# First attention: head norms summed by TensorE instead of VectorE

## The reference, cut to what matters

```python
xn = layernorm(x)
q = (xn @ Wq.T + bq)            # 16 heads of 16
k = (xn @ Wk.T + bk)            # 8 heads of 16
v = (xn @ Wv.T + bv)            # 8 heads of 16
q, k = rotary(q), rotary(k)     # turns pairs, keeps each head's length
n = sqrt(sum(h * h)) per head   # of q and of k
p = (h / max(n, 1e-6)) @ R.T    # R: 8 x 16, random features
feats = [sin(p), cos(p)] / 4
out = qp @ (kp^T v) per position, over heads
s = out @ Wo.T + bo
```

## Time and profile before

| | us |
|---|---|
| median of 3 runs (lowest, highest) | 1841.6 (1835.0, 1843.4) |
| the profiled execution, its span | 1837.6, 1835.8 |
| first attention, from the start to the last copy out of `psO` | 0 to 319.2 |
| DVE busy over the span | 1380.6 (75%) |
| PE busy over the span, weight loads | 1597.9 (87%), 1238.0 (67%) |

### The profile page before, as it was taken

One profiled execution on the slowest core, in us unless ns is written; L12 is line 12 of the kernel. 1 busy time (PEld: TensorE's weight loads), 2 busy tenths in 40 slices (PEclk: granted clock), 3 DMA queues, 4 the chain that ended last, 5 costly groups with the idle time before them and its releaser, 6 DMA issues. The chain is left out here.

```text
span 1835.8 us, 34559 instructions
## 1 busy us (share of the span) xinstructions
PE 1597.9 (87%) x9650; PEld 1238.0 (67%) x9650; DVE 1380.6 (75%) x3710; ACT 1031.0 (56%) x2457; POOL 667.8 (36%) x842
## 2 busy tenths in 40 slices
PE   6996886689954786999999999996899999988896
PEld 5885765579953563554555555544799999977775
DVE  7899998266657877999888888833666666667777
ACT  2664654256656660566676767674556666543443
POOL 2655687400027623111237667620000000056662
PEclk9998999789986995999999999998999999999998
DMA  9333456644435885432435545413864444355552
GB/s 343 130 87 85 106 146 167 205 137 133 133 116 168 290 306 149 99 74 61 106 97 156 160 142 171 128 61 122 274 201 133 133 134 133 117 166 164 169 165 75
DMA packets 279591, 272.72 MB, mean 149 GB/s; under 512 B 121769, under 2 KB 248426, under 8 KB 277356
## 3 DMA queue, kind: packets, MB, share of 16 engines
q1 hardware_dynamic: 255672, 215.41, 39.8%
q0 software_dynamic: 18432, 50.36, 9.0%
q10 hardware_dynamic: 5332, 4.96, 0.8%
HBM read 136.84 MB, written 133.69 MB: 147 GB/s over the span
## 5 line engine op out<-in xcount | busy, mean ns | idle before, releaser
L1890 ACT ACTIVATE ca_PT<-ca_psS 128x512 f32<-128x512 f32 (+3 forms) x768 | 336.3, 494 | 202.9 <-PE ca_psS L1927 197.8
L1430 POOL DMA_INDIRECT g_y<-ys_scratch,pos x128 | 125.0, 977 | 428.2 <-POOLq L73 357.0
L1806 DVE CUSTOM_DVE_ANT_0 ca_masked_row<-ca_psM,mask_row 128x384 f32<-128x384 f32 (+3 forms) x512 | 224.3, 486 | 44.4 <-PE ca_psM L1910 42.4
L1927 PE MATMUL ca_psS<-ca_QS,ca_KS 128*128 128x512 f32 (+1 forms) x480 | 174.7, 367 | 1.4 <-ACT ca_PT L1890 1.4
L1810 DVE TENSOR_REDUCE ca_part<-ca_psM 128x1 f32<-128x512 f32 x256 | 163.4, 685 | 16.1 <-PE ca_psM L1910 14.7
L1939 PE MATMUL ca_psO<-ca_PT,ca_VA 128*17 128x512 f32 (+3 forms) x1536 | 161.0, 491 | 6.0 <-ACT ca_OT L1882 5.9
L1910 PE MATMUL ca_psM<-ca_KS,ca_QS 126*128 126x512 f32 (+2 forms) x480 | 159.0, 379 | 6.5 <-DVE ca_part L1806 4.2
L797 PE MATMUL fa_psO<-fa_weighed,ident 128*128 128x256 f32 x512 | 127.9, 407 | 38.1 <-DVE fa_weighed L585 38.1
L1927 PEld LDWEIGHTS ca_psS<-ca_QS,ca_KS 128*128 128x128 f32 x480 | 90.2, 189 | 86.8 <-ACT ca_PT L1890 58.1
L391 POOL DMA_INDIRECT xs_scratch<-x_sb,pos x128 | 124.6, 973 | 55.9 <-ACT ca_PT L1890 34.1
L797 PEld LDWEIGHTS fa_psO<-fa_weighed,ident 128*128 128x128 f32 x512 | 101.7, 204 | 59.0 <-DVE fa_weighed L585 44.6
(11 more groups left out here) (271 smaller groups left out, 4638.5 us busy)
## 6 DMA issues: line engine op xcount, KB each, us to landing
xs_scratch<-fa_blank SPq DMA_DIRECT2D x32, 640.0 KB, 4.9
x_sb<-xs_scratch SPq DMA_DIRECT2D x143, 128.0 KB, 2.1
ys_scratch<-x_sb SPq DMA_DIRECT2D x143, 128.0 KB, 1.7
xs_scratch<-fa_blank SPq DMA_DIRECT2D x32, 384.0 KB, 6.4
spare<-qk_scratch SPq DMA_DIRECT2D x24, 512.0 KB
ca_QS<-qk_scratch SPq DMA_DIRECT2D x20, 512.0 KB, 6.1
ca_KS<-qk_scratch SPq DMA_DIRECT2D x20, 512.0 KB, 7.6
x_sb<-in_ffn SPq DMA_DIRECT2D x16, 608.0 KB, 4.5
```

The lines of the kernel that those rows point to most:

```text
L1430: pool.indirect_dma_start(y[:, t % R, k, :], None, y_dram, bass.IndirectOffsetOnAxis(pos[:, t, k:k + 1], 0)).then_inc(got[t % R], 16)
L1806: ins = dve.tensor_tensor_reduce(masked_row[:, (n * NU + u) % BANKS, h * w:(h + 1) * w], bank[:, h * w:(h + 1) * w], mask_row[:, CHUNK - w ...
L1890: act.activation(PT[:, s % PTS, h, off:CHUNK], psS[(GH * s + h) % BANKS][:, off:CHUNK], ACT.Exp)\
L1927: pe.matmul(psS[tile % BANKS][:, off:CHUNK], KS[slot][:, h, kt * P:(kt + 1) * P], QS[slot][:, h, c * CHUNK + off:(c + 1) * CHUNK], start=T ...
```

## The change

DVE's `square_norm` and its buffer `n2` go. ACT's Square moves from `take_qkv`, where it read `psQ`, to `keep_rotT`, where it reads the transposed rotated rows in `psR` right after the copy to `rotT`. PE's `random_projection` issues three more float32 matmuls: the squared transposed rows (128 x 128) against `heads`, a 128 x 8 block matrix of ones, into 24 further columns of `psP`. `keep_p` copies 216 columns instead of 192, and `norm` takes the sums from there and waits for `p_out` instead of `n2_done`. `heads` is made once by DVE, by a reduction of the identity matrix, before its first step. `project` no longer waits for ACT's squares. The diff, cut to its core:

```diff
@@ DVE @@
-            def square_norm(t, i, b):
-                dve.wait_ge(sq_done, t + 1)
-                dve.tensor_reduce(n2[:, i, :], sq[:, i % 2, :].rearrange("p (h d) -> p h d", d=D), AX.X, ALU.add)\
-                   .then_inc(n2_done, 1)
...
+            dve.wait_ge(ident_in, 16)
+            dve.tensor_reduce(heads[:, :], ident[:].rearrange("p (h d) -> p h d", d=D), AX.X, ALU.add).then_inc(heads_done, 1)
             in_steps(dve, (5, bounded_norm), (11, sine_sums), (5, inverse_norm), (8, in_turns), (11, centre), (8, whole_turns), (11, weigh),
-                     (8, fraction), (3, square_norm), (9, differences), first=BESIDE, beside=beside)
+                     (8, fraction), (9, differences), first=BESIDE, beside=beside)
@@ ACT @@
                 act.activation(qk[:, i % 2, :], psQ[:, 0:NQK], ACT.Copy).then_inc(qk_out, 1)
-                if late(t, 2):
-                    act.wait_ge(n2_done, t - 1)
-                act.activation(sq[:, i % 2, :], psQ[:, 0:NQK], ACT.Square).then_inc(sq_done, 1)
...
                 act.activation(rotT[:, i % 2, :], psR[:, 0:NQK], ACT.Copy).then_inc(rotT_out, 1)
+                act.activation(sq[:, i % 2, :], psR[:, 0:NQK], ACT.Square).then_inc(rotT_out, 1)
...
-                act.activation(p_sb[:, i, :, :].rearrange("p h f -> p (h f)"), psP[:, 0:QK_HEADS * RF], ACT.Copy).then_inc(p_out, 1)
+                act.activation(p_sb[:, i, :], psP[:, 0:NP + QK_HEADS], ACT.Copy).then_inc(p_out, 1)
...
-                    act.wait_ge(n2_done, t + 1)
+                    act.wait_ge(p_out, t + 1)
...
-                    act.activation(inv[:, some, :], n2[:, some, :], ACT.Sqrt).then_inc(norm_done, BATCHED)
+                    act.activation(inv[:, some, :], p_sb[:, some, NP:NP + QK_HEADS], ACT.Sqrt).then_inc(norm_done, BATCHED)
@@ PE @@
                 if t >= 1:
-                    pe.wait_ge(sq_done, t)
                     pe.wait_ge(qk_out, t)
...
                 for k in range(NQK // P):
-                    ins = pe.matmul(psP[:, k * 64:(k + 1) * 64], rotT[:, i % 2, k * P:(k + 1) * P], rblk[:],
-                                    start=k == 0, stop=True, skip_group_check=True)
+                    if k == 0:
+                        pe.wait_ge(rotT_out, t * 2 + 1)
+                    pe.matmul(psP[:, k * 64:(k + 1) * 64], rotT[:, i % 2, k * P:(k + 1) * P], rblk[:],
+                              start=k == 0, stop=True, skip_group_check=True)
+                pe.wait_ge(rotT_out, t * 2 + 2)
+                for k in range(NQK // P):
+                    at = NP + k * QHEADS
+                    ins = pe.matmul(psP[:, at:at + QHEADS], sq[:, i % 2, k * P:(k + 1) * P], heads[:, :],
+                                    start=False, stop=True, skip_group_check=True)
                 ins.then_inc(p_done, 1)
```

More of the change, by code:

```diff
@@ L415, in first_attention @@
         v = sb("v", [P, TILES, NV])
-        n2, inv = sb("n2", [P, POS_TILES, QK_HEADS]), sb("inv", [P, POS_TILES, QK_HEADS])
-        p_sb = sb("p_sb", [P, POS_TILES, QK_HEADS, RF])
+        NP, QHEADS = QK_HEADS * RF, P // D
+        inv = sb("inv", [P, POS_TILES, QK_HEADS])
+        p_sb, heads = sb("p_sb", [P, POS_TILES, NP + QK_HEADS]), sb("heads", [P, QHEADS])
         turns, whole = (sb(x, [P, 2, QK_HEADS, RF]) for x in ("turns", "whole"))
@@ L428, in first_attention @@
         (eps_done, root_done, rstd_done, xn_done, xT_done, hi_done, lo_done, logits_out, whi_done, wlo_done, qk_done, qk_out, v_done,
-         v_out, bias_part, rot_parts, rot_done, sq_done, n2_done, norm_done, norm_part, inv_done, rotT_done, rotT_out, p_done, p_out,
+         v_out, bias_part, rot_parts, rot_done, heads_done, norm_done, norm_part, inv_done, rotT_done, rotT_out, p_done, p_out,
          turns_part, turns_done, apart_done, sine_done, sines_done, A_done, centred, weighed_done, sums_done, out_done, ones_done) = (
@@ L432, in first_attention @@
                 "eps_done", "root_done", "rstd_done", "xn_done", "xT_done", "hi_done", "lo_done", "logits_out", "whi_done",
-                "wlo_done", "qk_done", "qk_out", "v_done", "v_out", "bias_part", "rot_parts", "rot_done", "sq_done", "n2_done", "norm_done",
+                "wlo_done", "qk_done", "qk_out", "v_done", "v_out", "bias_part", "rot_parts", "rot_done", "heads_done", "norm_done",
                 "norm_part", "inv_done", "rotT_done", "rotT_out", "p_done", "p_out", "turns_part", "turns_done", "apart_done", "sine_done",
@@ L546, in in_turns @@
                 i3 = inv[:, i, :].unsqueeze(2).broadcast_to([P, QK_HEADS, RF])
-                dve.scalar_tensor_tensor(turns[:, i % 2, :, :], p_sb[:, i, :, :], 0.15915494309189535, i3, ALU.mult, ALU.mult)\
+                dve.scalar_tensor_tensor(turns[:, i % 2, :, :], p_sb[:, i, 0:NP].rearrange("p (h f) -> p h f", f=RF), 0.15915494309189535, i3, ALU.mult, ALU.mult)\
                    .then_inc(turns_part, 1)
@@ L777, in transpose_rotated @@
                 if t >= 1:
-                    pe.wait_ge(rotT_out, t)
+                    pe.wait_ge(rotT_out, t * 2)
                 for k in range(NQK // P):
@@ L783, in random_projection @@
             def random_projection(t, i, b):
-                pe.wait_ge(rotT_out, t + 1)
-                if t >= 1:
+                if t == 0:
+                    pe.wait_ge(heads_done, 1)
+                else:
                     pe.wait_ge(p_out, t)
                 for k in range(NQK // P):
-                    ins = pe.matmul(psP[:, k * 64:(k + 1) * 64], rotT[:, i % 2, k * P:(k + 1) * P], rblk[:],
-                                    start=k == 0, stop=True, skip_group_check=True)
+                    if k == 0:
[7 more added lines that the diff above has]
+                                    start=False, stop=True, skip_group_check=True)
                 ins.then_inc(p_done, 1)
```

## The result

The changed kernel takes 1866.95 us (median of 4 runs, 1856.24 to 1873.39) against 1841.2 us of the kernel before on the same chip; the ratio is 1.0143 (1.0107 to 1.0178). The forecast was 1843.7 us, 1834 to 1853, with 0.11 for slower. A second series gave 1874.4 us (6 runs, 1862.74 to 1880.66) and 1.0163 (1.0128 to 1.0199). The profiled execution after took 1856.24 us at a mean granted clock of 0.939; the one before took 1837.6 us at 0.947.

The account below looks back on a forecast made before the run. PE was taken to set the pace up to step 17, DVE from the routing on. 1837.6 + 6.2 - 4.1 = 1839.7 us, 1843.7 against the median, range 1834 to 1853: no measurable change.

Parts of the forecast that it names:

- What of it lies on the path: PE's added pairs ahead of the routing: 14 x 0.645 = 9.0 us, less idle places and DVE's slack, 6.2 us lost.
- PE becomes the limit at every step: Rival: PE's step grows longer than DVE's, decided in steps 24 to 33; 19.9 us lost, 1861.5 us, chance 0.07.
- The place of the pairs: PE's queue in steps 4 to 17: six added pairs a tile delay the routing by 6.2 us, bounds 3.2 and 8.3.
- the second idle place: PE's 1.20 us wait ahead of 80.95 us for POOL's rotation, expected to absorb that much of the added pairs.
- the first place: PE's 0.98 us wait ahead of 55.13 us for a copy of logits, expected to absorb that much of the added pairs.
- DVE's reduction: Removing it from DVE, worth 0.46 us a step, was to gain 4.1 us over steps 18 to 34, bounds 2.3 and 7.8.
- The list of clear steps: Steps 18, 21, 22, 33 and 34, where DVE's reduction falls clear of POOL's rotation: 5 x 0.46 = 2.3 us gained.
- PE in the second part: After the routing starts, PE's step of 6.92 us was to be level with DVE's 6.87, limiting the gain to about 0.41.
- The waits added: PE's wait for the moved square and `norm`'s for `p_out`, taken as covered or already met; none priced.
- The rest: ACT's squares stay 32 at 491 ns, the stage's end passes on one for one, and `heads` costs nothing.

Follow-up runs that it names:

- e5: The changed kernel with `heads` padded by zeros to 128 columns; 1843.54 us, ratio 1.0034.
- e10: The changed kernel run once more, unaltered; six runs from 1862.7 to 1880.7 us, its profile of an execution of 1880.46 us.
- e1: The changed kernel with `heads` padded by zeros to 64 columns; 1863.68 us, ratio 1.010.
- e6: The kernel before with six extra unread 8-column pairs a tile in tiles 0 to 13 only; 1867.0 us, ratio 1.0152.
- h2: Tiles 0 to 15 summed by DVE as before, 16 to 31 by PE as in the change, `heads` padded to 128 columns; 1841.09 us, ratio 1.0008.
- e2: The changed kernel without the three new matmuls, the norm taken of a constant; 1833.48 us, ratio 0.9968.
- e9: The changed kernel with `heads` padded to 128 columns and 34 unread transposes early on PE; 1847.14 us, ratio 1.0057.
- h1: Tiles 0 to 15 summed by DVE as in the kernel before, 16 to 31 by PE as in the change; 1841.23 us, ratio 1.0017.
- e8: The kernel before with 34 unread transposes early on PE and no added pairs; 1839.09 us, ratio 1.0006.
- e4: The kernel before with six extra unread pairs a tile, 64 columns wide; 1848.15 us, ratio 1.0041.
- e3: The kernel before with six extra unread pairs a tile, 8 columns wide; 1877.95 us, ratio 1.020.

## Why the prediction was wrong

The step that failed is in "What of it lies on the path": the six pairs were priced at the clock of the earlier trace rows, 1.00 in the stretch before, and that price was multiplied by 14 as though the stretch would keep its clock. A lower clock was weighed only for steps 24 to 33, where the forecast named it as the point from which "PE becomes the limit at every step" decides. It fell in steps 4 to 17, where PE has no slack and every instruction of the stage pays, the old ones too: the records of `values` matmuls grow from 0.28 us to 0.41, and a whole step from 5.77 to 10.44 us (below).

**The place of the pairs**, +6.2 with bounds of 3.2 and 8.3: held. At a clock of 1.00 it is 7.4 us (e5). It lies above the value taken because the second idle place absorbed nothing: in e5 PE still waits 1.32 us for POOL's rotation there (at 84.99 below), and only the 0.98 of the first place is gone. 14 x 0.66 - 0.98 - 0.7 = 7.6 us.

**The clock**, not in the sum: in the first profile 17.5 - 7.4 = 10.1 us, in e10 40.1 - 7.4 = 32.7. `random_projection` comes once a step, so its starts give the step at either level. Timeline of PE, of the profile after, of e5 and of e10, in this order:

```profile
34.48 0.78 PE L786 MATMUL fa_psP<-rblk,fa_rotT 128*128 128x64 f32 x6
...
55.97 0.78 PE L786 MATMUL fa_psP<-rblk,fa_rotT 128*128 128x64 f32 x6
...
61.74 0.78 PE L786 MATMUL fa_psP<-rblk,fa_rotT 128*128 128x64 f32 x6
```

```profile
37.85 0.78 PE L786 MATMUL fa_psP<-rblk,fa_rotT 128*128 128x64 f32 x6
...
84.99 0.55 PE L775 MATMUL fa_psR<-ident,fa_rot 128*128 128x128 f32 x3 [1.32 <-POOL fa_rot L718]
```

```profile
37.68 1.38 PE L786 MATMUL fa_psP<-rblk,fa_rotT 128*128 128x64 f32 x6
...
48.12 1.38 PE L786 MATMUL fa_psP<-rblk,fa_rotT 128*128 128x64 f32 x6
```

One program takes 61.74 - 55.97 = 5.77 us for such a step at 1.00 and 48.12 - 37.68 = 10.44 at 0.50: of each us at the low level 1 - 5.77 / 10.44 = 0.447 us is lost. The 30.8 us of the first profile make 13.8. Its first projection starts 37.85 - 34.48 = 3.4 us ahead of e5's, which leaves 10.4 for the 10.1; what PE waits in either profile differs by 0.4 us. The 77.3 us of e10 make 34.6, and the 1.32 us that PE idles in e5 and not in e10 leave 33.2 for the 32.7. So the low clock accounts for what the place of the pairs leaves. The same working gives 23.7 us in e1 and 23.6 in e6, where 23.3 and 22.0 are to be explained; in h2, which has no added pair there, 10.6 less a start that is 3.6 us earlier than the kernel before's make 7.0 for the 6.8 measured.

**DVE's reduction**, -4.1 with bounds of 2.3 and 7.8: 2.4 to 3.3 us (after, e1, e5, e2), near the lower bound, but 0.9 in e9's profile, and in e10's the stretch is 1.8 us longer than before. `fraction` of steps 24 and 33 of the profile after, which answers to the earlier trace rows, and the two ways in which `weigh` goes, to the earlier trace rows:

```profile
215.76 2.29 DVE L581 TENSOR_TENSOR fa_weighed<-fa_A,fa_v 128x2048 f32<-128x2048 f32 x1
217.96 0.35 DVE L554 TENSOR_TENSOR fa_turns<-fa_turns,fa_whole 128x192 f32<-128x192 f32 x1
...
221.60 1.04 POOL L718 TENSOR_TENSOR fa_rot<-fa_rot_a,fa_rot_b 128x384 f32<-128x384 f32 x1
221.70 3.09 DVE L581 TENSOR_TENSOR fa_weighed<-fa_A,fa_v 128x2048 f32<-128x2048 f32 x1
...
282.68 0.34 DVE L554 TENSOR_TENSOR fa_turns<-fa_turns,fa_whole 128x192 f32<-128x192 f32 x1
```

The nine steps take 282.68 - 217.96 = 64.72 us, 7.19 each against 7.33 before: 0.14 us kept of 0.46, where 0.15 were counted. That part held; the shortfall lies outside it. Ahead of step 24 1.0 us came back where 1.8 were counted (steps 18, 21 and 22 as clear), and from step 33 on 0.2 where 0.9 were counted. The list of clear steps was also read too short: in step 25 the reduction ends at 208.82 + 0.54 = 209.36 us, ahead of POOL's next rotation at 209.48, and in steps 27, 29 and 31 it is alike.

What is stretched is not what was forecast. By the groups by line over the first attention the means of `differences` and `fraction` fell, from 1349 to 1311 and from 645 to 469 ns, and that of `weigh` rose from 2370 to 2559. `weigh` lasts 3.09 us where POOL's L718, begun 0.10 us ahead of it, is under way for its first 0.94 us, and 2.29 where no rotation runs: 0.80 us lost. The Trainium skill, "SBUF — State Buffer", section "SBUF: two separate sides", says that VectorE and GpSimd hold their shared port pair as an exclusive lock. The rows agree with that. That the rotation stands there because the reduction left the place free is read from the two timelines; no run tests it.

**PE in the second part** was forecast as level with DVE, 6.92 against 6.87 us. PE's timeline after:

```profile
225.41 3.62 PE L800 MATMUL fa_psO<-fa_weighed,ident 128*128 128x256 f32 x16
...
239.38 3.67 PE L800 MATMUL fa_psO<-fa_weighed,ident 128*128 128x256 f32 x16
...
247.08 3.72 PE L800 MATMUL fa_psO<-fa_weighed,ident 128*128 128x256 f32 x16 [0.80 <-DVE fa_weighed L581]
```

A step of PE is 247.08 - 239.38 - 0.80 = 6.90 us without its wait, as counted. In every other step PE no longer waits for `weigh`, in those between it does. So "PE becomes the limit at every step", whose 1861.5 us lies nearest to the result, is not what happened: it was placed in steps 24 to 33, and the loss is there before the routing starts.

**The waits added** were not priced, and one shows. ACT and DVE in step 36 of the profile after:

```profile
293.11 0.35 ACT L656 ACTIVATE fa_p_sb<-fa_psP 128x216 f32<-128x216 f32 x1 [1.34 <-PE fa_psP L791]
...
295.20 0.41 DVE L529 TENSOR_SCALAR fa_inv<-fa_inv 128x96 f32<-128x96 f32 x1 [0.44 <-ACT fa_inv L664]
```

`norm` stands behind `keep_p`, which waited for PE's new matmuls, and DVE waits 0.44 us for it; in the kernel before it had no wait there.

**The rest** held: ACT's squares moved at 487 ns, the shift passed on from `r_top` to the last copy to the span nearly one for one (e10: 40.1, 41.9 and 42.6 us), and `heads` costs nothing. With the place at 7.4 and the gain at 3.0 the sum would have been 1842.0 and 1846 against the median, which is near the eight common runs of e5.

## What to carry to other kernels

A clock of 1.00 read in the trace before belongs to the mix of matmuls that ran there; work that is moved onto a TensorE without slack should be priced at both levels, 0.65 and 1.24 us here, and the old work around it too, 5.77 and 10.44 us a step. Where PE sets the pace of a stage, its granted clock by window is the first thing to read after such a change, in more than one run: one program took 1856 to 1881 us by it. Padding the 8 columns with zeros to 128 won back most of the loss here, but could not beat the reduction on DVE, which costs the kernel only some 3 us in the profile of e2.

## What the runs showed of the chip

With PE busy throughout, the granted clock of one stage was 1.00 or 0.50, by the run and by whether six pairs a tile were added, and of what width. After one or more stops of 0.4 to 3.1 us it stayed at 0.50 for 7 us (h1), 16 us (e8) and 24 us (h2) without added pairs, 10 us (e9) with 128 columns, 3 (e4) and 61 us (e1) with 64, and 7 (after), 71 (e10) and about 30 and 40 us (e6, e3) with 8. That is one profile each: the pairs make long low stretches likely, but h2 shows that they are not needed for one. What in the pairs does it, their width, their data or their place, and what ends a low stretch, is not settled.

From the first fall on the records agree with the durations in the rows shown here. The Trainium skill, "TensorE: Matmul & The Clock Gate", section "Part 1: The HAM clock gate", warns that these records can be unreliable and that the gate has been seen stuck at a quarter of the pulses for 50 us and more. The 71 us of e10 agree in length, though at a half, and the warning holds for the start of every profile: up to the first fall the record says 1.00, while four transposes of the profile after take 1.12 us at 18.68, 1.11 at 26.04 and 0.66 at 32.10, so the first rise lies between the last two.

```profile
18.68 1.12 PE L747 MATMUL fa_psT<-ident,s 128*128 128x128 f32 x4 [6.94 <-DVE s L516]
...
26.04 1.11 PE L747 MATMUL fa_psT<-ident,s 128*128 128x128 f32 x4
...
32.10 0.66 PE L747 MATMUL fa_psT<-ident,s 128*128 128x128 f32 x4
```

By the same four transposes the rise of the kernel before comes between 34.03 (1.11 us) and 40.79 (0.65), that of e3, which up to there issues the same instructions on PE, ahead of 24.09 (0.66), and that of the changed kernel ahead of 24.14 in e10 and behind 26.04 in its first profile. So the moment differs by 10 us between executions of one instruction stream. The six profiles with the rise ahead of 25 us (e1, e3, e6, e8, e9, e10) all have the stop of 3 us ahead of 31 us, and none of the other eight has it.
